# Expert phase: weighted sums ahead of the next slots' halves on VectorE, second transposes later on TensorE

## The reference

```
for c in range(2):                                   # first and second choice of each token
    xb   = slots of each expert                      # 8 experts x 640 slots x 256
    hmid = relu(xb @ W1[e] + b1[e])                  # 640 x 1024
    yb   = hmid @ W2[e] + b2[e]                      # 640 x 256
    y    = y + prob * yb[slot of the token]
```

## Time and profile before

| | |
|---|---|
| median of 3 runs | 2661.23 us (2660.52 to 2666.82) |
| profiled execution | 2662.25 us |
| its span | 2660.5 us, 41009 instructions |
| mean granted clock of TensorE | 0.976 |
| TensorE busy | 2469.9 us, 93% |
| VectorE busy | 1817.0 us, 68% |
| ScalarE busy | 1213.9 us, 46% |
| GpSimd busy | 1332.6 us, 50% |

### The profile page before, as it was taken

The page is one execution under the profiler, slowest core; times in us unless marked ns, Lnnn a source line. Parts: engine busy times, 40 slices in busy tenths (PEclk is TensorE's granted clock), DMA queues, the critical chain, the costliest instruction groups (busy, mean ns, idle before and its releaser), DMA issues. The chain is left out here.

```text
span 2660.5 us, 41009 instructions
## 1 busy us (share of the span) xinstructions
PE 2469.9 (93%) x15764; PEld 2191.6 (82%) x15764; DVE 1817.0 (68%) x3855; ACT 1213.9 (46%) x2127; POOL 1332.6 (50%) x805
## 2 busy tenths in 40 slices
PE   7899998599999999999999979999999579999998
PEld 6788787488888998888889967777777479999998
DVE  6888887566667666666667566666666556666665
ACT  4777777433333333333333246656556233333332
POOL 2443433355566666556666525666666423333333
PEclk9999999899999999999999989999999789999999
DMA  3222211420000000100000132222222034334331
GB/s 126 70 72 82 79 61 63 167 103 27 29 25 24 25 25 25 33 27 26 25 25 21 35 100 82 92 95 92 86 79 62 19 131 134 126 132 134 125 125 56
DMA packets 135362, 190.39 MB, mean 72 GB/s; under 512 B 13378, under 2 KB 104039, under 8 KB 135040
## 3 DMA queue, kind: packets, MB, share of 16 engines
q1 hardware_dynamic: 121344, 157.34, 18.2%
q0 software_dynamic: 13824, 30.44, 3.5%
HBM read 123.20 MB, written 72.12 MB: 73 GB/s over the span
## 5 line engine op out<-in xcount | busy, mean ns | idle before, releaser
L651 POOL TENSOR_TENSOR prob<-prob,softmax_small 128x1024 f32<-128x1024 f32 x65 | 124.1, 1909 | 236.9 <-DVE softmax_small L574 236.9
L1925 POOL TENSOR_TENSOR m_hl<-m_hf,m_hh 128x512 fp32r<-128x512 f32 x112 | 168.5, 1516 | 146.1 <-ACT m_hh L1633 145.9
L2161 ACT ACTIVATE e_hf<-e_ps_z,e_b 128x640 f32<-128x640 f32 x128 | 101.8, 795 | 269.5 <-PE e_ps_z L102 269.1
L2271 POOL DMA_INDIRECT out<-e_ys,slot_token x80 | 79.0, 987 | 280.1 <-DVE e_ys L2230 267.6
L102 PE MATMUL e_ps_y<-e_w_h,e_hl 128*128 128x256 f32 x640 | 185.0, 289 | 28.2 <-DVE e_ys L2230 28.2
L102 PE MATMUL e_ps_y<-e_w_h,e_hh 128*128 128x256 f32 x640 | 182.0, 284 | 0.0
L102 PE MATMUL e_ps_y<-e_w_l,e_hh 128*128 128x256 f32 x640 | 182.0, 284 | 0.0
L1937 POOL DMA_INDIRECT xbuf_d<-xn,scatter_rows x128 | 150.2, 1173 | 45.3 <-issue 38.9
L102 PE MATMUL e_ps_z<-slotsT_h,w_l 128*128 128x320 f32 x512 | 159.7, 312 | 0.9 <-DVE slotsT_l L2208 0.9
L102 PE MATMUL e_ps_z<-slotsT_l,w_h 128*128 128x320 f32 x512 | 159.5, 311 | 0.0
L102 PE MATMUL e_ps_z<-slotsT_h,w_h 128*128 128x320 f32 x512 | 159.4, 311 | 0.0
(11 more groups left out here) (291 smaller groups left out, 8972.1 us busy)
## 6 DMA issues: line engine op xcount, KB each, us to landing
shared_x<-in_x SPq DMA_DIRECT2D x32, 512.0 KB, 5.0
shared_xT<-xT_d SPq DMA_DIRECT2D x64, 256.0 KB, 4.6
new_w1T<-in_W SPq DMA_DIRECT2D x16, 1024.0 KB
new_w2T<-in_W SPq DMA_DIRECT2D x16, 1024.0 KB, 5.7
xbuf_d<-new_w1T SPq DMA_DIRECT2D x16, 650.0 KB, 8.4
slots<-xbuf_d SPq DMA_DIRECT2D x16, 650.0 KB, 6.3
xn_d<-xn SPq DMA_DIRECT2D x32, 256.0 KB, 2.5
xT_d<-shared_xT SPq DMA_DIRECT2D x32, 256.0 KB, 2.5
```

Source lines behind the costliest of these rows:

```text
L651: e.tensor_tensor(p[:], p[:], sm[:, 3].unsqueeze(2).broadcast_to([P, HEADS, 2 * P]), ALU.mult).then_inc(*prob_made(g))
L1925: e.tensor_tensor(hl[:, t], hf[(HC * C + t) % NZ][:], hh[:, t], ALU.subtract).then_inc(*h_low(C, t))
L2161: e.activation(hf[(HC * i + t) % NHF][:].rearrange("p (s n) -> p s n", s=2), ps_z[t % 2][:, :, 0:HALF], ACTF.Relu, bias=b1[:, i % E, t:t + ...
L2271: e.indirect_dma_start(io["out"], bass.IndirectOffsetOnAxis(ap=token[i % 2][:, b:b + 1], axis=0), ys[:, b], None, bounds_check=NT - 1, oob ...
```

## The change

On TensorE the second transposes move from behind block 1 to behind block 3 of the down products. On VectorE the bias sums become five separate steps with a signal each, and a weighted sum waits for the bias sum of its own block only. The turn of a round is reordered: bias and weighted sum of block 0, first halves of the next slots, bias and weighted sum of block 1, the other three bias sums, the small slot operations, weighted sums 2 and 3, second halves, weighted sum 4. GpSimd's, ScalarE's and SyncE's lists stay as they are, and so does the arithmetic.

```
-        rows_made = signal("e_rows_made", rounds)
+        rows_made = signal("e_rows_made", rows_of)
...
                 down(i, 1, 1)
-                if i + 1 < ROUNDS:
-                    transpose_slots(i + 1, 1)
                 for b in range(2, SB):
+                    if i + 1 < ROUNDS and b == SB - 1:
+                        transpose_slots(i + 1, 1)
                     down(i, b, 0)
                     down(i, b, 1)
...
-            def add_bias(i):
+            def add_bias(i, b):
                 dve.wait_ge(*rows_in.at(i, SB - 1))
                 dve.wait_ge(*prob_made.at(i))
                 dve.wait_ge(*b2_in.at(0))
-                for b in range(SB):
-                    x = e.scalar_tensor_tensor(rows[:, b], b2[:, i % E], prob[i % 2][:, b:b + 1], rows[:, b], ALU.mult, ALU.add)
-                x.then_inc(*rows_made(i))
+                e.scalar_tensor_tensor(rows[:, b], b2[:, i % E], prob[i % 2][:, b:b + 1], rows[:, b],
+                                       ALU.mult, ALU.add).then_inc(*rows_made(i, b))
 
             def weigh(i, b):
                 dve.wait_ge(*y_done.at(i, b))
-                dve.wait_ge(*rows_made.at(i))
+                dve.wait_ge(*rows_made.at(i, b))
...
                 if i + 1 < ROUNDS:
                     rest_w1(i + 1)
+                add_bias(i, 0)
+                weigh(i, 0)
+                if i + 1 < ROUNDS:
                     rest_slots(i + 1, 0)
-                add_bias(i)
-                weigh(i, 0)
+                add_bias(i, 1)
                 weigh(i, 1)
+                for b in range(2, SB):
+                    add_bias(i, b)
+                if i + 1 < ROUNDS:
+                    slot_tokens(i + 1)
+                weigh(i, 2)
+                weigh(i, 3)
                 if i + 1 < ROUNDS:
                     rest_slots(i + 1, 1)
-                    slot_tokens(i + 1)
-                for b in range(2, SB):
-                    weigh(i, b)
+                weigh(i, 4)
```

## The result

The changed kernel takes 2625.41 us (median, 2624.51 to 2626.72), the kernel before 2662.86 us over four executions: 37.5 us less, ratio 0.9858 with a 95% interval of 0.9841 to 0.9875. The forecast was 2624 us. The profiled execution took 2626.72 us, with a span of 2624.9.

A forecast was written before the change was run, and what follows sets the result against it. TensorE, busy 93%, was taken as bound by waits for VectorE's late weighted sums, and by clock drops behind them. 30.9 + 7.7 - 1.3 = 37.3 us off 2661.2 gave 2624 us, range 2617 to 2634.

The forecast's parts named there:

- Term 1: TensorE's wait at block 2 for block 0's weighted sum goes: 2.06 us a round, 30.9 us over 15 rounds.
- Term 2: Half-speed clock stretches in blocks 2 to 4 go with the waits: 1.53 us in five rounds, 7.7 us.
- Rival 1: The clock drops stay, perhaps a rhythm of the chip's own; only terms 1 and 3 count: 2632 us, chance 8%.
- Term 3: Blocks 2 to 4 all run at the slower pace, 8.59 not 8.27 us, set behind transposes without a wait: 1.3 us lost.
- Slack: Block 0's weighted sum ends 0.7 us before block 2 needs it; second halves have 1.8 us to spare under block 4.
- Rival 2: weigh(0) or weigh(1) is late after all, a smaller wait in the old one's place: 2636 or likelier 2630 us, chance 9%.
- Rival 3: The next round's first gate product waits for the second halves behind the later transposes: slower, 2676 us, chance 2%.
- rival 4: No net change: waits move to another bank, block 3 or 4 needing a sum behind the bias sums: 2660 us, chance 3%.

The follow-up runs named there:

- wait filled: Kernel before plus 14 extra products that nothing reads where block 2 waits for its bank, VectorE's order unchanged: 2658.16 us, ratio 0.997.
- halves first: Changed kernel with the first halves of the next slots back ahead of bias and weighted sum of block 0: 2635.05 us, ratio 0.9886.
- warm start: Changed kernel plus 16 and 10 extra products nothing reads, ahead of the phase's first and second transposes: 2625.16 us against 2625.79 unedited.
- transposes alone: Kernel before with only the second transposes moved behind block 3, VectorE's order as before: 2701.58 us, ratio 1.013.
- VectorE's order alone: Changed kernel with the second transposes back behind block 1, new VectorE order and split bias signal kept: 2632.03 us, ratio 0.987.
- bias split: Kernel before with each bias sum right ahead of its weighted sum and its own signal, all else in place: 2633.8 us, ratio 0.988.
- sums late: Changed kernel with first halves and all five bias sums ahead of block 0's weighted sum, late transposes kept: 2669.45 us, ratio 1.0013.

## Why the prediction was right

**The bound.** Right: one wait, placed by VectorE's order. With the sum late again the time is that of before, although the transposes stay later; with the sum early and the transposes where they were, the phase is 7 us above the new one.

**Term 1**, 30.9 us. By the trace the two transposes hold TensorE 0.14 us and not 0.20, so 15 x (2.26 - 0.14) = 31.8 us.

**Term 2**, 7.7 us. Right, and shown by itself: 7.9 us with the wait filled. Rival 1, drops with a rhythm of their own, has fallen three times: none with the wait gone, none with it filled, and six at uneven distances when the wait is 1.92 us, in rounds as long as before (31.2 to 33.0 us). The advice of the Trainium skill, TensorE: Matmul & The Clock Gate, "Why this matters for your kernels", which would have had the drops remain, does not hold here: waits of 1.88 us were enough, five times in fifteen. I had written that the granted clock would read 1.00 from the first round on. It does so only from the middle of round 0: that round's up products run at 0.82, before and after the change, because the phase starts at half clock.

**Term 3**, 1.3 us against. All 15 rounds run at the slower pace, as taken: 8.57 us for the 72 products between the first and the second transposes, 2.91 us for the 24 behind them. The loss is 0.4 us more than counted, since before the faster pace also lasted over the next round's first 24 products. But the reason I gave was wrong. In the kernel with the halves first, block 4 ran at the faster pace behind transposes without a wait in 3 of 15 rounds (2.81 us in place of 2.91), and in round 0 of the warm start so did all 72 products (8.26 us in place of 8.57). What decides the pace stays open.

Sum by these numbers: 31.8 + 7.7 - 1.7 = 37.8 us, against 38.2 in the phase and 37.5 between the medians.

**Slack.** Forecast 0.7, 1.8 us and no wait at block 2 and the next round's first up product; read 0.73 and 1.8. The halves-first kernel turns the first into a wait where it should. Rivals 2, 3 and 4 did not come about. The turn of rival 4, a wait moved to another bank, is what the transposes alone would have brought; it needs the second halves ahead of weigh(2), which the new order avoids.

**Where luck had a part.** The loss of term 3 came out near the number for a reason that does not hold, and its error of 0.4 us and that of 0.9 us in term 1 go opposite ways. Not luck but a gap: I gave the split of the bias sums no term of its own, and it is the largest part, 1.6 of the 2.1 us a round, and with it the clock.

## What to carry to other kernels

When a fast engine waits for a slow one's queue, list what stands in that queue ahead of the instruction waited for, and ask of each who wants it next: here 1.6 us of bias sums that nobody needed yet were most of 38 us. A signal for a whole group of blocks makes the first wait for the last; one for each block costs nothing that shows. Price such a wait together with the clock: what the idle time takes off TensorE afterwards was a fifth of the gain, and a kernel with the same lateness but no idleness is how to tell them apart. The same edit can change its sign with its neighbours: the transposes' move was worth 7 to 8 us with the new order and cost 34 without it.

## What the runs showed of the hardware

How often a wait of TensorE was followed by a 3.41 us stretch at 1.2 GHz, over the 15 turns of a kernel:

| idle time | kernel | followed by a drop |
|---|---|---|
| 0.2 to 0.5 us | wait filled, VectorE's order alone, bias split, halves first | 0 of 15 in each |
| 1.68 us | transposes alone, block 4 | 0 of 15 |
| 1.88 us | before | 5 of 15 |
| 1.92 us | sums late | 6 of 15 |
| 2.11 us | transposes alone, block 2 | 7 of 15 |

The waits of 1.68 and 1.88 us stand right behind two transposes, those of 1.92 and 2.11 us behind products of block 1. Each of the 18 drops began between 0 and 1.5 us after TensorE had resumed, so the slow stretch need not begin with the first product behind the wait. Equal waits at equal places have the effect in one round and not in the next, and what picks the round is not shown here, so a count over all rounds is needed before a drop is put down to a wait. A drop costs 1.5 us here (10.12 against 8.59 us for the same 72 products), nearly as much as the wait ahead of it. I had not expected that products without any wait between them have two paces at a granted clock of 1.00: 72 of them take 8.27 or 8.59 us.
